# Cross-attention added to 32 batches: values made by sides, queries made transposed, sums one step behind the probabilities, 20 slots, stores by halves

## The reference, cut to what matters

```
def reference(x, ctx_1024, Wq, Wk, Wv):      # x, ctx_1024: (32, 512, 512); W: (512, 512)
    q, k, v = x @ Wq.T, ctx @ Wk.T, ctx @ Wv.T          # split in 16 heads of 32
    probs = softmax(q k^T / sqrt(32))                   # per batch and head, 512 x 512
    att = (probs v), heads joined                       # (32, 512, 512)
    tgt2 = att[0]                                       # of batch 0 alone
    return x + tgt2                                     # added to all 32 batches
```

## Time and profile before

| | |
|---|---|
| median of 3 runs (lowest, highest) | 252.85 us (251.79, 254.68) |
| profiled execution: its time | 252.51 us |
| its span (first to last instruction) | 250.7 us |
| TensorE matmul busy | 176.3 us, 70% |
| DVE busy | 112.3 us, 45% |
| ACT busy | 94.7 us, 38% |
| POOL busy | 79.5 us, 32% |
| mean granted TensorE clock | 0.905 of full |
| DMA: moved, mean rate | 71.64 MB, 286 GB/s |

### The profile page before, as it was taken

The page is one execution under the profiler, slowest core; times in us unless marked ns, Lnnn a source line. Parts: engine busy times, 40 slices in busy tenths (PEclk is TensorE's granted clock), DMA queues, the critical chain, the costliest instruction groups (busy, mean ns, idle before and its releaser), DMA issues.

```text
span 250.7 us, 5252 instructions
## 1 busy us (share of the span) xinstructions
PE 176.3 (70%) x2104; PEld 98.9 (39%) x2104; DVE 112.3 (45%) x216; ACT 94.7 (38%) x217; POOL 79.5 (32%) x70
## 2 busy tenths in 40 slices
PE   7999899999777584977577758777758667661000
PEld 7655354444445241633344325433434424440000
DVE  0322224463357366435544564456665637565000
ACT  2312225350457244407444443166445544540000
POOL 1000000000007805900391039202921940777800
PEclk9999999999999797799977986999999979998555
DMA  7999999984302501999990009999992799503998
GB/s 236 409 401 421 423 422 422 420 358 182 161 4 118 220 0 44 359 344 427 421 408 16 0 4 314 414 426 421 425 420 103 298 420 420 209 3 146 420 426 346
DMA packets 11560, 71.64 MB, mean 286 GB/s; under 512 B 1168, under 2 KB 1168, under 8 KB 3728
## 3 DMA queue, kind: packets, MB, share of 16 engines
q1 hardware_dynamic: 11536, 71.31, 70.5%
HBM read 37.75 MB, written 33.55 MB: 284 GB/s over the span
## 4 chain that ended last, share of the span: by engine, by line
issue 58%; POOL 31%; DMA 4%; SPq 1%; POOLq 1%
POOL slots L302 31%; DMA slots<-in_x_dram 4%; POOLq L54 1%; SPq L251 0%; SPq L250 0%; SPq L249 0%; SPq L248 0%; POOLq L300 0%
## 5 line engine op out<-in xcount | busy, mean ns | idle before, releaser
L302 POOL TENSOR_TENSOR slots<-slots,att_right 128x512 f32<-128x512 f32 x64 | 78.8, 1270 | 156.7 <-ACT att_right L663 156.7
L729 DVE TENSOR_REDUCE neg_max<-bank 128x1 f32<-128x512 f32 x64 | 43.2, 686 | 69.8 <-PE bank L385 69.8
L656 ACT COPY probs_t<-bank 128x512 f32<-128x512 f32 x62 | 36.3, 586 | 69.7 <-PE bank L397 66.5
L397 PE MATMUL bank<-ident,probs 128*128 128x128 f32 x256 | 43.7, 296 | 4.6 <-ACT probs L648 2.5
L648 ACT ACTIVATE probs<-bank,neg_max 128x512 f32<-128x512 f32 x64 | 44.5, 696 | 3.8 <-DVE neg_max L729 3.8
L756 DVE TENSOR_TENSOR slots<-slots,bank 128x512 f32<-128x512 f32 x64 | 42.4, 673 | 0.7 <-PE bank L451 0.7
L385 PE MATMUL bank<-k_t,q_t 32*64 32x512 f32 x256 | 38.8, 682 | 0.0
L397 PEld LDWEIGHTS bank<-ident,probs 128*128 128x128 f32 x256 | 30.5, 149 | 14.3 <-issue 7.7
L451 PE MATMUL bank<-ident,att_t 128*128 128x128 f32 x64 | 11.4, 304 | 20.5 <-DVE slots L756 13.0
L440 PE MATMUL bank<-probs_t,v 128*32 128x64 f32 x992 | 21.5, 230 | 3.9 <-issue 2.8
L440 PEld LDWEIGHTS bank<-probs_t,v 128*32 128x32 f32 x992 | 16.6, 115 | 18.7 <-issue 10.7
(11 more groups left out here) (46 smaller groups left out, 92.2 us busy)
## 6 DMA issues: line engine op xcount, KB each, us to landing
slots<-in_x_dram SPq DMA_DIRECT2D x32, 1024.0 KB, 17.4
out_dram<-slots SPq DMA_DIRECT2D x28, 1024.0 KB, 11.5
out_dram<-slots SPq DMA_DIRECT2D x8, 512.0 KB, 3.5
ctx_raw<-in_ctx_dram SPq DMA_DIRECT2D x1, 1024.0 KB, 4.9
wq_raw<-in_L_xattn_Wq_dram SPq DMA_DIRECT2D x1, 1024.0 KB, 9.3
wv_raw<-in_L_xattn_Wv_dram SPq DMA_DIRECT2D x1, 1024.0 KB, 13.2
wk_raw<-in_L_xattn_Wk_dram SPq DMA_DIRECT2D x1, 768.0 KB, 7.1
wk_raw<-in_L_xattn_Wk_dram SPq DMA_DIRECT2D x1, 256.0 KB, 2.7
```

The lines of the kernel that those rows point to most:

```text
L302: nc.gpsimd.tensor_tensor(xs, xs, att_right[:, H % 2, :, :], ALU.add).then_inc(right_added, 1)
L397: last = nc.tensor.transpose(turn_bank(H, u)[:, t * P:(t + 1) * P], probs[:, u % 2, t * P:(t + 1) * P], ident[:, :])
L656: nc.scalar.copy(probs_t_of(H, u), turn_bank(H, u).rearrange("p (t n) -> p t n", t=T)).then_inc(act_turned_out, 1)
L729: nc.vector.tensor_reduce(neg_max[:, H % 2, u:u + 1], bank[:, u % S_BANKS, :], AX_X, ALU.max, negate=True).then_inc(max_ready, 1)
```

## The change

- Values are made by sides: `v_left` (columns 0 to 255, 16 matmuls of 128 x 256) first and `v_right` (16 more) later, woven into half 0, in place of 16 matmuls of 128 x 512.
- The sides change hands. The left side is turned to a turn bank, copied by ACT to a single `att_left` and added by POOL; the right side is turned to `BACK_BANK` and added by DVE. `turn_left(H)` stands at the end of half H, `turn_right(H)` in half H+1 behind `lay_out_sums`.
- The queries are made transposed: `make_queries` multiplies with Wq as the resting operand in 16 matmuls of 128 x 128 and gives `q_t` at once; ACT scales and copies them. The second transposing, its copy and one `q_t` buffer fall away.
- `PT_SLOTS` is 4 in place of 6. A turned unit is copied when the sums of the unit four before are done. In half 0 `sum_group` follows the probabilities within the half; halves 0 and 1 have their own order, in which all their sums are done at their end.
- On DVE `invert_sums` now stands ahead of the two maxima that it stood behind or between.
- 20 slots in place of 19, and every group is stored in two stores of 0.5 MB, half H by half H. A reload waits for both halves and stands 3 groups behind the stores of an odd half.

The diff, cut to its core:

```
-    SLOTS = 2 * GROUPS + 3
+    SLOTS = 2 * GROUPS + 4
-    PT_SLOTS = 6
+    PT_SLOTS = 4
-        TURNS = [(0, 0), (0, 1), (0, 2), ("x0", 1), (0, 3), (0, 4), ("x0_t", 1), (0, 5), (0, 6), (0, 7)]
+        TURNS = [(0, 0), (0, 1), (0, 2), (0, 3), (0, 4), (0, 5), (0, 6), (0, LEFT_SIDE), (0, 7)]
+        TURNS += [("x0", 1), (1, 0), (1, 1), (1, 2), (1, 3), ("x0_t", 1), (1, 4), (1, 5), (1, 6), (1, 7), (1, LEFT_SIDE)]
...
         def sums_before(H, u):
-            before, unit = divmod(H * UNITS + u - PT_SLOTS, UNITS)
-            return 0 if H == 0 else sums_through(before, unit // 2)
+            replaced = H * UNITS + u - PT_SLOTS
+            return 0 if replaced < 0 else replaced // 2 + 1
...
             LAG = 3
             LOADS = T * GROUPS
-            for g in range(SPLIT):
-                store_half(0, g)
-            for n in range(LOADS):
...
+            for H in range(HALVES):
+                for g in range(GROUPS):
+                    store_half(H, g)
+                    half_before, group_before = divmod(H * GROUPS + g - LAG, GROUPS)
+                    n = half_before // 2 * GROUPS + group_before + SLOTS
+                    if half_before >= 0 and half_before % 2 == 1 and n < LOADS:
+                        reload(n)
...
+            def make_queries(ps, g):
+                for c in range(C):
+                    last = mm(ps[:, g * P:(g + 1) * P], wq_t[:, c, g * P:(g + 1) * P], x0_t[:, c, :],
+                              start=(c == 0), stop=(c == C - 1))
+                return last
...
             def turn_left(H):
                 pe.wait_ge(att_t_ready, sums_through(H, 1))
-                if H == 0:
-                    emptied(pe, "q", 1)
-                else:
-                    pe.wait_ge(left_added, added_through(H - 1, GROUPS - 1))
-                turn_rows(bank[:, BACK_BANK, :]).then_inc(back_ready, 1)
+                turn_bank_free(H, LEFT_SIDE)
+                turn_rows(turn_bank(H, LEFT_SIDE)).then_inc(turned, 1)
             def turn_right(H):
                 pe.wait_ge(att_t_ready, sums_through(H, HG - 1))
-                turn_bank_free(H, RIGHT_SIDE)
-                turn_rows(turn_bank(H, RIGHT_SIDE)).then_inc(turned, 1)
+                if H > 0:
+                    pe.wait_ge(right_added, added_through(H - 1, GROUPS - 1))
+                turn_rows(bank[:, BACK_BANK, :]).then_inc(back_ready, 1)
```

More of the change, by code:

```diff
@@ L384, in score_pair @@
                     rows, s = slice(i * DK, (i + 1) * DK), i % 2
-                    last = mm(bank[s * QH:(s + 1) * QH, (u + i // 2) % S_BANKS, :], q_t[rows, H // 2 % 2, g, queries],
+                    last = mm(bank[s * QH:(s + 1) * QH, (u + i // 2) % S_BANKS, :], q_t[rows, g, queries],
                               k_t[rows, g, :], start=True, stop=True, tile_position=(i * DK, s * QH))
@@ L548, in _ @@
             gather_x0(job_bank("x0", 0), 0).then_inc(bank_filled, 1)
+            turn("wq_t", 1)
+            for c in range(C):
+                key_chunk(3, c)
+            turn("wq_t", 2)
+            emptied(pe, "x0", 0)
+            bank_free("x0_t", 0)
+            transpose_x0(job_bank("x0_t", 0)).then_inc(bank_filled, 1)
+            turn("wq_t", 3)
             pe.wait_ge(wv_loaded, 16)
             turn("wv_t", 0)
-            emptied(pe, "x0", 0)
-            bank_free("x0_t", 0)
-            transpose_raw(job_bank("x0_t", 0)).then_inc(bank_filled, 1)
@@ L707, in _ @@
             copy_probs(0, 6)
-            empty("q", 1)
-            for H in range(1, HALVES):
+            copy_left(0)
+            copy_probs(0, 7)
+            exponent(1, 0)
+            exponent(1, 1)
+            copy_probs(1, 0)
+            exponent(1, 2)
+            copy_probs(1, 1)
+            exponent(1, 3)
+            copy_probs(1, 2)
+            exponent(1, 4)
+            copy_probs(1, 3)
+            exponent(1, 5)
+            copy_probs(1, 4)
+            exponent(1, 6)
+            copy_probs(1, 5)
+            exponent(1, 7)
+            copy_probs(1, 6)
+            copy_probs(1, 7)
+            copy_left(1)
+            empty("q_t", 1)
+            for H in range(2, HALVES):
                 half(H)
             copy_probs(HALVES - 1, 7)
-            copy_right(HALVES - 1)
+            copy_left(HALVES - 1)
         @block.vector
@@ L759, in half, with add_before, add_after @@
             def half(H):
                 j = H // 2 + 1
-                more = H + 1 < HALVES
-                normalize(H - 1, 2)
+                first, more = H % 2 == 0 and j < T, H + 1 < HALVES
+                def add_before(i):
+                    if H == 2:
+                        add_right(1, 2 + i)
+                    elif H > 3:
+                        add_right(H - 2, 5 + i)
+                def add_after(i):
+                    if H > 2:
+                        add_right(H - 1, i)
+                    elif i < 3:
+                        add_right(1, 5 + i)
```

410 lines of the change are left out of this document (201 added, 209 removed).

## The result

The changed kernel takes 200.04 us (median of 4 runs, 199.70 to 200.46) against 252.32 us for the kernel before in the same comparison. The ratio is 0.7947, with a 95% interval of 0.7898 to 0.7997. The forecast was 197 us in a range of 187 to 216. The profiled execution has a span of 197.6 us, where 195 was worked out.

The account below looks back on a forecast made before the run. The order in TensorE's list, not transfers, was taken as the bound: first half out, period and tail. Stores ending at 192 to 193.5, with 2 added, gave span 195; 1.8 around it made 197 us, range 187 to 216.

Parts of the forecast that it names:

- First scores: Start of the kernel: smaller value matmuls and fewer copy waits bring first scores at 33.6 us in place of 36.66.
- nearest-row choice: Query passes on TensorE: priced at 0.11 us each, like the nearest profiled transposes' operand loads; 3.5 us a tile.
- First half out: Halves 0 and 1: `turn_right(0)` at 60.4, first store at 61 for 78.42, 17 us earlier; `turn_right(1)` near 82.3.
- The period: One plain half on TensorE: 13.7 us for 21.0; 3.3 more with queries, 3.8 more with x0.
- the walk: One half followed step by step through TensorE's list from the turning of unit 3 at 0, to 13.65 us.
- Four buffers: Copy of unit 4 waits for sum 0, covered by scores and sum 1; uncovered, up to 1 us a half.
- The chain does not close up: Rival, 18 in 100: four buffers, one `att_left` and busy DVE leave about 3 us a half idle; 215 us.
- Only the ends gain: Rival, 7 in 100: periods stay at 25 and 21 us, only start and end gain; 229 us.
- Mixed transfers at the low rate: Rival, 10 in 100: loads mixed with stores go at 253 GB/s; 222 us, or 205 with a few more dips.
- Each store pays its landing: Rival, 1 in 100: 64 stores and 12 loads wait for one another, ending near 315 us.
- The last half: After unit 3 of half 7 at 168.2: right side turned at +13, additions end at 187, stores at 192 to 193.5.
- The allowance of 2 us: End of the span: 2 us added for gaps in the walk and the dip of mixed loads and stores.

Follow-up runs that it names:

- c1: The changed kernel with SP's first store held until unit 6 of half 1 is turned (75 us in place of 62.5); 199.84 us.
- a6: The changed kernel with 19 slots for 20 and 6 turned-unit buffers for 4; 202.54 us, against 202.82 with 19 slots and 4 buffers.
- e1: The kernel before with all stores of 0.5 MB, half by half, 19 slots, compute untouched; 243.16 us against 251.15.
- a2: The changed kernel with loads 20 to 31 bringing only two of four rows, 6.3 MB less; 197.45 us.
- b1: The changed kernel with DVE's copies of x0 and x0_t one to three steps earlier in DVE's list; 197.45 us.
- b3: As b1, and DVE makes its first five right additions of halves 3 and 5 while TensorE makes the queries; 195.82 us.
- a1: The changed kernel with the 8 groups of tile 3 stored whole, when half 7 is added; 206.57 us.
- a4: The changed kernel with the left side of halves 2 to 7 turned back between units 6 and 7 again; 203.80 us.
- e2: The kernel before with DVE's inverse of the sums ahead of the maxima in halves 2 to 7; 251.02 us against 251.15.
- e3: As e2, and the left side of halves 2 to 7 turned back behind unit 7 or the second laid sums; 239.33 us.

## Why the prediction was right

Point by point, by its own steps.

- **First scores** at 33.6; measured 34.89, 1.3 later. The queries begin at 28.54 and their 32 passes last to 32.19: 0.114 us each, where 0.11 was taken (the load of the resting operand) of a range of 0.107 to 0.22. The nearest-row choice was right, and the queries take 3.65 us a tile.

```profile
28.54 3.81 PE L332 MATMUL bank<-x_t,wq_t 128*128 128x128 f32 x32
32.19 1.04 PE L314 MATMUL bank<-ident,wv_raw 128*128 128x128 f32 x8
...
34.89 1.95 PE L374 MATMUL bank<-k_t,q_t 32*64 32x512 f32 x16
```

- **First half out.** `turn_right(0)` at 60.4, measured 60.99; first store 61, measured 62.51; `turn_right(1)` at 82.3, measured 82.78. The 17 us were 16. But the prediction counted the first store as a term of its own, and c1 shows that its date is worth nothing; what counts, by the dates, is the chain behind it.

- **The period.** 13.7 us, measured 13.67. These are the starts in half 6 of the kernel after, answering to the earlier trace rows:

```profile
154.52 1.09 PE L374 MATMUL bank<-k_t,q_t 32*64 32x512 f32 x8
...
155.24 0.66 DVE L775 TENSOR_TENSOR slots<-slots,bank 128x512 f32<-128x512 f32 x1
...
155.54 0.43 PE L426 MATMUL bank<-ident,recip 128*32 128x64 f32 x16
...
156.64 0.65 PE L457 MATMUL bank<-ident,att_t 128*128 128x128 f32 x4 [0.67 <-issue]
...
157.13 0.60 PE L386 MATMUL bank<-ident,probs 128*128 128x128 f32 x4
...
157.66 0.65 PE L446 MATMUL bank<-probs_t,v 128*32 128x64 f32 x32
...
159.85 0.65 PE L446 MATMUL bank<-probs_t,v 128*32 128x64 f32 x32
...
168.19 1.09 PE L374 MATMUL bank<-k_t,q_t 32*64 32x512 f32 x8
```

 The score pair stood at 0.59 in the walk, so its zero is 153.93: laid sums at 1.61, the right side at 2.71 for 1.95, sum 0 at 3.73 for 3.4, sum 1 at 5.92 for 5.6, and the next score pair 13.67 behind this one. The right side is the place where the walk read the order wrongly: the last addition that frees its bank was not long done, as the prediction had it, but begins at 155.24 and ends at 155.90, which is 1.97 in the walk. The 0.7 us between this end and the turning the profile puts down to no engine. From there the half runs 0.1 to 0.4 us late and catches up at its last two units, which take 1.06 us together where 1.24 was walked. With queries or x0, 17.0 and 17.5 were walked; POOL's starts lie 16.8 to 16.9 apart. The last two are 11.95 apart, under the 13.5 that the prediction named as the least. The full clock was forecast and came: 1.00 over 60 to 175 us.

- **Four buffers** cost nothing, as walked: a6. **The chain does not close up** is out: no idle of 3 us a half. (Its 215 us were 20 us on the span of 195; on the time of 197 they are 217.) **Only the ends gain** is out: the periods fell. **Mixed transfers at the low rate** is out: the dips are there, three times 4 us, and behind each the rate is 399 to 424 GB/s again. **Each store pays its landing** is out: e1, and the earlier trace rows had said so. The rule of the Trainium skill, "DMA: Bandwidth & Descriptors", section "Bandwidth", on transfers of at least 1 MiB stands there beside a table of loads issued by GpSimd. For stores of 0.5 MB that SP issues and that queue behind each other it does not hold here: from 151 to 176.6 us they go at 413 GB/s.

- **The last half.** Last additions at 187, measured 186.5; the turned right side, at +13 by the walk, stands at 180.43. The full rate ends at 194.6 us, where 192 to 193.5 was worked out and 2 us were added for gaps and dips. Then 3 us follow with hardly a byte, which the sum had not counted (the last two numbers of a row are the DMA share and GB/s):

```profile
193.00:194.00 1.00, 0.00 (x0) 0.00 (x0) 0.00 (x0) 0.00 (x0) 0.00 (x0) 0.50 0.99 406
194.00:195.00 1.00, 0.00 (x0) 0.00 (x0) 0.00 (x0) 0.00 (x0) 0.00 (x0) 0.50 0.60 238
195.00:196.00 1.00, 0.00 (x0) 0.00 (x0) 0.00 (x0) 0.00 (x0) 0.00 (x0) 0.50 0.07 29
196.00:197.00 1.00, 0.00 (x0) 0.00 (x0) 0.00 (x0) 0.00 (x0) 0.00 (x0) 0.50 0.04 16
```

 In the kernel before this end is about 1 us. So the 2.6 us by which the span of 197.6 is over 195 are this end, which the last term of the sum left out; the terms before it were right within 1.5 us. The other 0.4 us of the miss is what lies around the span: 2.1 to 2.9 us in the four executions, where 1.8 was taken from the kernel before. The trace shows what the end is: a share of 0.06 is one of 16 engines, and from 195.2 to 196.7 us the last packets of 4 KB land one by one, 0.16 us apart, while all other engines are done. So one engine had 1.5 us of work left over. It is the same in a2, b1 and b3, with two engines in c1, and there is no such remainder in a1, a4, e1 and the kernel before. Why the work is uneven there was not tried. The allowance of 2 us was used up, by estimate, by the small stores (413 GB/s, not 420: over the 29.4 MB behind 84 us 1.2 us) and by three dips where one was allowed for.

- **What was argued too simply** is that the inverse and the left side are two waits to be taken away one by one. The walk of the whole half had the right sum; the parts are not a sum. Taken alone in the old order the first is worth 0.1 us, both 11.8; from the new order the first costs 11.0 and the second 3.8 to put back.

## What to carry to other kernels

Where engines wait for each other in fixed lists, cost a reordering by walking one whole period with start-to-start times from the trace; a wait that is taken out alone can come back at the next thing the same engine is late with, as in e2. Then look at where the transfers run out of work: here a free stretch of the adding engine was worth 1.6 us and the date of the first store nothing, and at the end it paid to store each half as it became complete. Buffers that the walk shows covered can be given up for a slot of data, and one slot was worth 2.8 us.

## What the runs showed of the hardware

When loads begin within a stream of stores, the transfers move little for some 4 us at full busy share, and then run at the usual rate with loads and stores still mixed. The earlier trace rows have it once at 253 GB/s. In the changed kernel it happens each time the reloads begin: 261 GB/s over 90 to 94 us, 273 over 116 to 120 and 294 over 138 to 142, at shares of 1.01, 1.03 and 0.92, and 403, 399 and 424 in the 4 to 8 us behind. An estimate from these rates is 4 us lost in all. In the dips a load's packet of 8 KB takes a mean of 0.52, 0.53 and 0.44 us, and 0.31 to 0.33 us behind them. In b3, where the gap ahead of the second reloads is closed, the second dip is not there either: 94 to 126 us runs at 409 to 425 GB/s. So part of what b3 gains may be this dip. Why a dip comes and why it ends was not tried.

The kernel before lost more than the idle time itself when TensorE stood still: behind the left side's wait of 1.85 us the clock was granted at 1.2 GHz (0.50 of full over 203 to 206 us), and a score pair took 1.98 for 1.09. In e3, where such waits are 5.9 us for e2's 12.5, the clock over 100 to 200 us is 0.97 for 0.91; how much of its 11.7 us is clock and how much is the wait was not separated.
